# Cross-attention of a decoder layer: exponentials in place, four buffers for the scores with the top ones removed, value products transposed, and a new order of the work in every engine's step

## The reference, cut to what matters

```
q = heads(layernorm(x) @ Wq.T + bq)      # 16 heads of 32, 100 queries
k = heads(ctx @ Wk.T + bk);  v = heads(ctx @ Wv.T + bv)   # 722 keys
scores = q @ k.T / sqrt(32)
top_scores, top_idx = top_k(scores, 32)
w = softmax(top_scores)
out = sum(w * v[top_idx])
x = x + out @ Wo.T + bo
x = x + layernorm(x) @ M + bias
```

## Time and profile before

| | us |
|---|---|
| median of 3 runs | 2792.08 |
| lowest, highest | 2772.25, 2794.88 |
| profiled execution | 2798.57 |
| its span, first to last instruction | 2796.8 |
| mean granted TensorE clock of the span | 0.898 of full speed |

### The profile page before, as it was taken

How to read it: one execution, slowest core, us unless ns; L and a number is a source line. 1 busy time by engine, 2 the same in 40 slices (tenths; PEclk the granted TensorE clock), 3 DMA queues, 4 the chain that set the end, 5 groups by cost and what they waited for, 6 DMA issues and landing times. The chain is left out here.

```text
span 2796.8 us, 47371 instructions
## 1 busy us (share of the span) xinstructions
PE 2325.4 (83%) x16760; PEld 1898.0 (68%) x16760; DVE 2033.7 (73%) x3866; ACT 1411.8 (50%) x3040; POOL 1014.8 (36%) x912
## 2 busy tenths in 40 slices
PE   3788788788878758899898898898899988988987
PEld 2556556555655447787787777777778877877875
DVE  4544544554454218899899899899898988998996
ACT  3222222122222125767667667667666666666663
POOL 3344335334533122343333343343333333333421
PEclk9898898889888779999999899999999999999987
DMA  4000000000000230000000000010000000000000
GB/s 157 7 19 9 9 18 9 9 9 18 9 9 12 79 97 14 25 15 14 25 19 15 15 28 15 15 28 14 15 26 17 15 16 28 15 15 23 14 1 7
DMA packets 37617, 63.03 MB, mean 23 GB/s; under 512 B 4014, under 2 KB 20542, under 8 KB 37420
## 3 DMA queue, kind: packets, MB, share of 16 engines
q1 hardware_dynamic: 35836, 56.28, 6.7%
q0 software_dynamic: 1584, 4.30, 0.5%
HBM read 53.99 MB, written 6.55 MB: 22 GB/s over the span
## 5 line engine op out<-in xcount | busy, mean ns | idle before, releaser
L1236 DVE MATCH_REPLACE8 ca_W<-ca_top,ca_W 128x722 f32<-128x722 f32 (+1 forms) x624 | 553.4, 894 | 0.0
L1227 DVE MAX8 ca_top<-ca_W 128x8 f32<-128x722 f32 (+1 forms) x624 | 536.3, 897 | 2.6
L883 POOL TENSOR_TENSOR ca_E<-ca_E,ca_S 128x722 f32<-128x722 f32 (+1 forms) x208 | 357.3, 1738 | 306.0 <-ACT ca_S L1088 305.9
L983 PE MATMUL ca_pO<-ca_V,ca_PT 128*128 128x64 f32 (+1 forms) x2496 | 347.1, 295 | 77.5 <-ACT ca_ctxT L1127 77.2
L983 PEld LDWEIGHTS ca_pO<-ca_V,ca_PT 128*128 128x128 f32 (+1 forms) x2496 | 334.8, 207 | 104.8 <-ACT ca_PT L1110 76.3
L865 POOL TENSOR_TENSOR ca_KL<-ca_K,ca_KH 128x384 fp32r<-128x384 f32 (+1 forms) x128 | 114.0, 891 | 508.9 <-ACT ca_KH L1081 508.9
L873 POOL TENSOR_TENSOR ca_cL<-ca_raw,ca_cH 128x768 fp32r<-128x768 f32 (+1 forms) x64 | 110.5, 1726 | 337.1 <-ACT ca_cH L1064 337.1
L1215 DVE MAX8 ca_top<-ca_S 128x8 f32<-128x722 f32 (+1 forms) x208 | 181.3, 901 | 58.0 <-ACT ca_S L1105 55.4
L88 PE MATMUL ca_pF<-ca_cH,ca_WkH 128*128 128x338 f32 (+1 forms) x512 | 194.3, 380 | 22.9 <-POOL ca_cL L873 22.9
L964 PE MATMUL ca_pT<-ca_ident,ca_E 128*128 128x128 f32 (+1 forms) x1248 | 190.4, 295 | 17.0 <-POOL ca_E L883 16.9
L1088 ACT ACTIVATE ca_S<-ca_W,ca_shift 128x722 f32<-128x722 f32 (+1 forms) x208 | 185.1, 890 | 38.6 <-DVE ca_W L1236 26.3
(11 more groups left out here) (204 smaller groups left out, 5256.4 us busy)
## 6 DMA issues: line engine op xcount, KB each, us to landing
ca_raw<-in_ctxT SPq DMA_DIRECT2D x32, 384.0 KB, 3.7
ca_raw<-in_ctxT SPq DMA_DIRECT2D x32, 338.0 KB, 3.0
sa_xin<-in_x SPq DMA_DIRECT2D x16, 200.0 KB
sa_xres<-in_x SPq DMA_DIRECT2D x16, 200.0 KB
x_scratch<-sa_x SPq DMA_DIRECT2D x16, 200.0 KB
ca_xin<-x_scratch SPq DMA_DIRECT2D x16, 200.0 KB
out<-ca_x SPq DMA_DIRECT2D x16, 200.0 KB
sa_E<-in_WQ SPq DMA_DIRECT2D x12, 256.0 KB, 13.2
```

The lines of the kernel that those rows point to most:

```text
L883: pool.tensor_tensor(E[r][0:t.rows, :], E[r][0:t.rows, :], S[r][0:t.rows, :], ALU.subtract).then_inc(p_ready, 1)
L983: last = pe.matmul(out, PT[:, k, 0:t.rows], rhs, start=k == 0, stop=k == KC - 1)
L1227: n_of[t.i] = order.mark(dve.max(eight, w[rows, :]))
L1236: ins = dve.match_replace(w[rows, :], eight, (w if k else S[r])[rows, :], REMOVED)
```

## The change

- **Buffers.** `E` is gone. `exps` writes exp(S) over S, `exps_left` exp(W) over W, GpSimd subtracts W from S into S, and the transposes read S. `W` has four buffers. `exps` now needs the first MATCH_REPLACE8 of its tile to have read S (semaphore `removed`); `keep_scores` needs the transposes of the tile four back.
- **Values.** V is stationary (32 columns), PT moves; the result comes out transposed, straight in head strips of a PSUM tile, `NUM`. A product of 1/Z (broadcast over 32 columns) with the identity puts the reciprocals beside it, `DEN`. For each group of four heads `keep_output` copies both to `NR`, and one multiplication on GpSimd (`place_output`) writes `ctxT`; the rest tile's is VectorE's. `normalise`, `output_T`, `On` and `late_tile` are gone.
- **Moved to GpSimd:** the shifts (`shifts`), 1/Z as a power of -1 (`inverse`), the low half of q (`query_low`).
- **Order.** ScalarE does `exps` at the end of its step, behind the second slices. TensorE starts with the first score in every step, both tiles of `last` do their values in the same step, and the projections of x stand in the middle. Output projection s = 1, statistics s = 3, `xn` and its transpose s = 4, product with M s = 5, store s = 6; for the next batch statistics s = 1, `xn` and transpose s = 2, q s = 3, split of q s = 5. `PLAN` moves slices 4, 11 and 13 behind. `xin` is loaded ahead of the context. q has a buffer of its own, `qT`.

The diff, with 8 columns of indent taken off, without the semaphore declarations, the setup and the row work whose new place stands above, and with most removed lines cut (they stand in the kernel above):

```diff
-    PLAN = [([12, 13], []), ([], [0, 1]), ([2], [3]), ([4, 5], [6]), ([], [7, 8]), ([9], [10]), ([11], [])]
+    PLAN = [([12], [13]), ([], [0, 1]), ([2], [3, 4]), ([5], [6]), ([], [7, 8]), ([9], [10]), ([], [11])]
...
-E = [sb(f"E{r}", [128, KV]) for r in range(RING)]
-W = [sb(f"W{r}", [128, KV]) for r in range(2)]
+W = [sb(f"W{r}", [128, KV]) for r in range(RING)]
...
+def group_of(t):
+    if t.rest:
+        return GROUPS - 1
+    return t.g if t.t == 2 else None
...
-            load_context(b, 0)
+            if not tiles:
+                load_context(b, 0)
             need(sp, xn1_ready, b.count(1, 1))
             need(sp, xb_ready, b.count(1, 1))
             sp.dma_start(xin[:, :], batch_of(x1_dram, b, 1)).then_inc(x_in, 16)
+            if tiles:
+                load_context(b, 0)
             load_context(b, 1)
...
+    def shifts(tb, tp, t):
+        r, rows = ring(t, tp), slice(0, t.rows)
+        pool.wait_ge(peaked, tb.count(NT, t.i + 1))
+        settle(pool)
+        pool.tensor_scalar(shift[rows, r:r + 1], top[r][rows, 0:1], -SCALE, None,
+                           ALU.mult).then_inc(shift_ready, 1)
+    def weights(tb, tp, t):
+        r, rows = ring(t, tp), slice(0, t.rows)
+        pool.wait_ge(e_ready, tb.count(NT, t.i + 1))
+        pool.wait_ge(f_ready, tb.count(NT, t.i + 1))
+        pool.tensor_tensor(S[r][rows, :], S[r][rows, :], W[r][rows, :], ALU.subtract).then_inc(p_ready, 1)
+    def inverse(tb, tp, t):
+        r, rows = ring(t, tp), slice(0, t.rows)
+        ob, oi = before(tb, t, RING)
+        need(pool, o_mm, parts_done(ob, Tile(oi)))
+        pool.wait_ge(z_ready, tb.count(NT, t.i + 1))
+        pool.tensor_tensor(rZ[rows, r:r + 1], Z[rows, r:r + 1], minus_one[rows, :], ALU.pow).then_inc(rz_ready, 1)
+    def place_output(tb, tp, t):
+        n = group_of(t)
+        if n is None or t.rest:
+            return
+        if n == 0:
+            need(pool, y_mm, tb.count(1, 0))
+        pool.wait_ge(o_kept, tb.count(GROUPS, n + 1))
+        pool.tensor_tensor(ctxT[:, n, :], NR[:, 0, :], NR[:, 1, :], ALU.mult).then_inc(ot_ready, 1)
+    def query_low(bn):
+        pool.drain()
+        for h in range(4):
+            rows, cols = slice(DH * h, DH * h + DH), slice(T * h, T * h + T)
+            pool.wait_ge(q_hi, bn.count(5, h + 1))
+            need(pool, q_lo, bn.count(5, h))
+            pool.tensor_tensor(QL[rows, :, cols], qT[rows, :, :], QH[rows, :, cols].bitcast(F32),
+                               ALU.subtract).then_inc(q_lo, 1)
...
+            first, second = (slices(s, part, b, par, tiles, nxt) for part in range(2))
+            for x in last:
+                weights(*x)
+            for x in last:
+                inverse(*x)
+            for x in cur:
+                shifts(*x)
...
+            if s in (1, 4) and nxt:
+                context_low(bn, 2 * (s // 3) + 1)
+            if s == 5 and nxt:
+                query_low(bn)
+            for x in first + second:
+                if SLICES[x[2]][1] == "K":
+                    key_low(*x)
+            for x in last:
+                place_output(*x)
+            if s in (0, 3) and nxt:
+                context_low(bn, 2 * (s // 3))
...
+        r = ring(t, tp)
         pe.wait_ge(pt_ready, tb.count(NT, t.i + 1))
...
+        pe.wait_ge(rz_ready, tb.count(NT, t.i + 1))
         if t.i == 0:
             pe.wait_ge(kv_out, tb.count(NSL, NSL))
+        if t.rest:
+            pe.wait_ge(o_kept, tb.count(GROUPS, 3))
+        elif t.t == 0:
+            need(pe, o_kept, tb.count(GROUPS, max(t.g - 1, 0)))
+        settle(pe)
+        if t.rest:
+            n = t.rows
+            pe.matmul(pO[3 * DH:128, DEN:DEN + n], rZ[0:n, r:r + 1].broadcast_to((n, DH)), ident[0:n, 0:n],
+                      start=True, stop=True)
+            for g in range(4):
+                at = NUM + REST * g
+                for k in range(KC):
+                    last = pe.matmul(pO[3 * DH:128, at:at + REST], V[tp][:, k, 128 * g + 3 * DH:128 * g + 128],
+                                     PT[:, k, REST * g:REST * g + REST], start=k == 0, stop=k == KC - 1)
+            last.then_inc(o_mm, 1)
+            return
+        at = T * (t.g % 2)
+        for _, cols, to, g, q in t.blocks():
+            pe.matmul(pO[to:to + DH, DEN + at + q.start:DEN + at + q.stop],
+                      rZ[:, r:r + 1].broadcast_to((128, DH)), ident[:, cols], start=True, stop=True)
         for k in range(KC):
...
+            for _, cols, to, g, q in t.blocks():
+                last = pe.matmul(pO[to:to + DH, NUM + at + q.start:NUM + at + q.stop],
+                                 V[tp][:, k, 128 * g + to:128 * g + to + DH], PT[:, k, cols],
+                                 start=k == 0, stop=k == KC - 1)
+                if k == KC - 1:
+                    last.then_inc(o_mm, 1)
     def body(b, par, tiles, prev, nxt):
         bn = b.next()
         for s in range(7):
             cur, last, coming = tiles_at(s, b, par, tiles, prev, nxt)
...
+            if coming:
                 score(*coming[0])
...
             for x in slices(s, 0, b, par, tiles, nxt):
                 project(*x)
             if last:
                 weights_T(*last[0])
...
+            if s == 1 and prev:
+                pe.wait_ge(ot_ready, b.count(GROUPS, 0))
+                for c in range(CC):
+                    ins = pe.matmul(pX[0:T, :], ctxT[:, c, :], WoT[:, c, :], start=c == 0, stop=c == CC - 1)
+                ins.then_inc(y_mm, 1)
+            if s == 3 and nxt:
                 pe.wait_ge(x1T_ready, bn.count(1, 1))
                 for o in range(CC):
                     for c in range(CC):
...
                 ins.then_inc(q_mm, 1)
...
+            if s == 5 and prev:
+                pe.wait_ge(x2T_ready, b.count(1, 0))
+                for c in range(CC):
+                    ins = pe.matmul(pX[0:T, :], xT[:, c, :], M[:, c, :], start=c == 0, stop=c == CC - 1)
+                ins.then_inc(f_mm, 1)
+            if last:
+                values(*last[0])
+            if len(coming) > 1:
+                score(*coming[1])
+            if len(last) > 1:
+                weights_T(*last[1])
+            for x in slices(s, 1, b, par, tiles, nxt):
+                project(*x)
...
+            if len(last) > 1:
+                values(*last[1])
...
         r, rows = ring(t, tp), slice(0, t.rows)
+        ob, oi = before(tb, t, RING)
         act.wait_ge(picked, tb.count(NT, t.i + 1))
...
+        act.wait_ge(shift_ready, tb.count(NT, t.i + 1))
+        act.activation(W[r][rows, :], W[r][rows, :], ACT.Exp, bias=shift[rows, r:r + 1],
                        scale=SCALE).then_inc(f_ready, 1)
+        need(act, rz_ready, ob.count(NT, oi + 1))
         act.activation(top[r][rows, :], top[r][rows, :], ACT.Exp, bias=shift[rows, r:r + 1],
                        scale=SCALE, accum_out=Z[rows, r:r + 1]).then_inc(z_ready, 1)
     def exps(tb, tp, t):
         r, rows = ring(t, tp), slice(0, t.rows)
+        act.wait_ge(removed, tb.count(NT, t.i + 1))
+        act.wait_ge(shift_ready, tb.count(NT, t.i + 1))
+        act.activation(S[r][rows, :], S[r][rows, :], ACT.Exp, bias=shift[rows, r:r + 1],
+                       scale=SCALE).then_inc(e_ready, 1)
+    def keep_scores(tb, tp, t):
         ob, oi = before(tb, t, RING)
         need(act, pt_mm, ob.count(NT, oi + 1))
...
         act.wait_ge(s_mm, tb.count(NT, t.i + 1))
         act.activation(S[ring(t, tp)][0:t.rows, :], scores[0:t.rows, :], ACT.Copy).then_inc(s_ready, 1)
     def keep_weights_T(tb, tp, t):
...
+        need(act, o_mm, parts_done(tb, t, before=True))
         act.wait_ge(pt_mm, tb.count(NT, t.i + 1))
         act.activation(PT[:, :, 0:t.rows], chunks(pT[:, 0:KC * 128], KC)[:, :, 0:t.rows],
                        ACT.Copy).then_inc(pt_ready, 1)
...
+    def keep_output(tb, tp, t):
+        n = group_of(t)
+        if n is None:
+            return
+        need(act, ot_ready, tb.count(GROUPS, n))
+        act.wait_ge(o_mm, parts_done(tb, t))
+        src = pO[:, 0:4 * T].rearrange("p (a g q) -> p a g q", a=2, g=2)[:, :, n % 2, :]
+        out = NR[:, :, :]
+        if t.rest:
+            src, out = (x[3 * DH:128, :, 0:4 * REST] for x in (src, out))
+        act.activation(out, src, ACT.Copy).then_inc(o_kept, 1)
...
+            if s in (1, 4) and nxt:
+                context_high(bn, 2 * (s // 3) + 1)
+            if s == 5 and nxt:
+                need(act, s_mm, b.count(NT, NT - 1 if tiles else 0))
...
+                    act.activation(QH[rows, :, T * h:T * h + T], qT[rows, :, :], ACT.Copy).then_inc(q_hi, 1)
+                need(act, s_mm, b.count(NT, NT if tiles else 0))
+                act.activation(chunks(RH[3 * DH:128, :], 4)[:, :, 0:REST], qT[3 * DH:128, :, T - REST:T],
                                ACT.Copy).then_inc(q_hi, 1)
...
             for x in slices(s, 0, b, par, tiles, nxt):
                 keep(*x)
             if last:
                 keep_weights_T(*last[0])
...
```

(40 more changed lines are left out.)

264 lines of the change are left out of this document (67 added, 197 removed).

## The result

The changed kernel takes **2956.03 us** (median of 4 runs, 2945.27 to 2964.36), the kernel before in the same comparison 2793.48 (2772.25 to 2796.31): a ratio of 1.060, 95% interval 1.054 to 1.066. I had forecast 2828 in a range of 2640 to 2900. The direction was right, the size was not: 163 us slower where I had 36, and outside the range.

What follows compares the result with a forecast made beforehand. The ring through three queues was to bound the kernel: 106.5 us plus 4.5 for the clock, 111 a batch, 3 more than before. Fifteen batches (+45) less 9 fixed gave +36, 2835, as median 2828 us; range 2640 to 2900.

Steps and rivals of the forecast that it cites:

- VectorE, `W`, GpSimd: Cross-attention batch: VectorE's work falls to 92.3 us, its wait for `W` goes, GpSimd's work rises to 60 us.
- Values per tile: TensorE's new value product: 1.1 us for a full tile instead of 1.45, 3.0 us for the rest tile.
- rival 4: Pauses in s1, s4, s6 cost the clock (8.6 us) and strips are dear (6 x 1.0): 121 us a batch, 2975 us; chance 0.13.
- The ring: Loop through ScalarE, GpSimd and TensorE queues, closed by exps at the step's end, sets the pace while VectorE waits.
- steps 3 and 5: Ring lengths at full clock of s3, with q before the values, 16.1 us, and s5, with the spectral product, 14.6 us.
- step 4: Ring length of s4 at full clock: 17.0 us, with the second raw piece landing late and two K slices.
- I take 4.5: Clock addition to a batch: 4.3 us at the granted 0.93, 8.6 if the low level's share doubles; 4.5 chosen.
- the sum: The seven steps' ring lengths at full clock added up: 106.5 us a batch, above VectorE's 92.3.
- TensorE's 57 us: TensorE's part of the 106.5 us ring, growing by 4.3 us at the granted clock of 0.93.
- the tail: Sign from the profile before: after 3.27 us idling the tail's spectral product took 5.37 us instead of 3.68.
- the first rival: The ring is slack and VectorE paces: a batch of 96 to 101 us, 2600 to 2690 us; chance 0.25.
- the second: Second rival: the ring holds but is shorter, 107.7 us a batch, 2785 us, no change; chance 0.27.

Runs made afterwards that it cites:

- c1: Changed kernel with exps behind the second score's copy (a1) and the output projection ahead of step 1's first transposes (a3): 2879.48 us, ratio 1.034.
- c2: c1 with the q projection also moved to the head of step 4 and the product with M to the head of step 6: 2798.10 us, ratio 1.005.
- b1: Kernel before, with only exps of the current pair moved to the end of ScalarE's step: 2786.81 us, ratio 1.000.
- a1: Changed kernel with exps right behind the copy of the second score instead of at the end of ScalarE's step: 2897.26 us, ratio 1.040.
- d1: Changed kernel with the three projections moved as in c2, exps left at the end of the step: 2849.15 us, ratio 1.023.
- a9: Changed kernel with 16 dummy products in TensorE's pauses of steps 1, 4 and 6: 2886.56 us, ratio 1.039.
- a2: Changed kernel with 32 dummy products in TensorE's pauses of steps 1, 4 and 6: 2928.02 us, ratio 1.051.
- a3: Changed kernel with the output projection moved ahead of the first transposes in step 1, into TensorE's pause: 2900.20 us, ratio 1.041.
- e1: c2 with ScalarE rounding the second context piece behind the first score copy in steps 1 and 4: 2749.90 us, ratio 0.989.

## Why the prediction was wrong, point by point

- **VectorE, `W`, GpSimd:** right. 93.5 us a batch against 92.3, no wait for `W`, GpSimd 54.7 against 60.
- **Values per tile:** about right. At full clock a tile's 28 instructions take 1.3 us (2031.41 to 2032.73), forecast 1.1; the rest tile's 48 products 1.7 to 1.9, forecast 3.0 with its sums. The Trainium skill (TensorEngine Tiling (Array Packing), Key Properties) says that a change of the tiling mode drains the engine. The rows put a small bound on it: the last value product ends at 2032.81 by its row, and the score behind it starts at 2032.73; the score's second product starts 0.27 us after its first, where the later ones follow 0.17 apart. A change back costs 0.1 us at most here. So of rival 4's price the 6.0 us for dear strips did not come.
- **The ring:** right in its path, and in its length where TensorE had no pause (steps 3 and 5, within 0.3 us). In step 4 I had the second context piece in place 5.3 us into the step and `values` at 6.9; it was 5.4 and 7.1. Step 3 gave back a member's duration when q went (c1 to c2). What it lacked: it is a ring only as long as nothing else is longer, as b1 and the misses of a1, c1, c2 and d1 say.
- **The term that failed is the clock's**, "I take 4.5". The table's excess over the sum is 12.2 us a batch. a9 gave 5.2 of it back by filling three pauses, nearly all in steps 1 and 6. Another 2.6 lie in step 4 and 1.4 in step 2, where a9 leaves the products slow; the first goes away in a2's step 4, the second in a3's step 2, each time with the same products at full clock. Together 9.2 us: the 8.6 that I had put under the fourth rival, not the 4.5. My working spread the loss over TensorE's 57 us at the old mean of 0.93. But pauses and slow products aren't spread: what TensorE waits for, GpSimd's subtraction, is the release of its own part of the ring, so every slow product behind the pause is on the path. I had written that rival 4 decides where the clock goes below 0.88; it was 0.87, and 2975 us was its price; that 2956 came so near it is partly luck, since half of what that rival added was the strips, and it had no term for the next point.
- **The rest, some 3 us a batch:** 6 times in thirteen batches, at the turn of the loop, TensorE stands 2.8 us with nothing shown that it waits for, 1.3 us a batch. The kernel before has that too (17.2 us, 6 times), and my sum left it out. Of the changed kernel:

```profile
PE ca_pS L88 <- issue: 16.9, 6, 3.1
```

  Another 1.2 us lie in step 0, and its thirteen turns say where: five have a granted clock of 1.00 and take 13.7 us, against my 14.1; the eight others have 0.74 to 0.89 and take 15.1 to 18.0, six of them right behind that stop of the loop. So this too goes with the clock, as far as reading shows; no run took it away. Some 0.5 us stay open.
- **The chances:** 0.13 for a case at or near what came, and a range cut at 2900 though half of that rival was at 2890. I had listed no sign against it: nothing in the profile of before spoke for a high clock beside pauses of 4 to 5 us, and the tail, spoke for a low one. Two small slips: 15 x (-7) - 9 from 2792 gives 2678 for the first rival, not 2690, and the second comes to 2779, not 2785.

Edits interact, so their gains don't add: `exps` gave 59 us alone, 21 behind the projection (a3 to c1) and nothing in the kernel before, q and M 81 behind those, while the reciprocal gave 36 us in e1's order and nothing that can be told in the changed kernel.

## What to carry to other kernels

Sum an in-order design as a ring through its queues, step by step, and then ask where on that ring TensorE stands idle: the products right behind the pause are the ones that run slow, and they are on the path, so price them one by one at the low level and not with a mean clock. Put independent products (a projection, here) into the pause rather than behind what ends it; that takes them off the ring. It keeps the clock only if the waits that are left are short: two of 1.4 and 1.8 us were enough to lose it again in a3. A filler must be shorter than the pause. An edit that is free in one order can be worth 59 us in another, so measure each move in the order that is to be kept, and read step by step where its gain came from: a3's total was as expected, and its steps were not.

## What the runs showed of the hardware

- After an idle time of 4.6 to 4.8 us the granted clock is at the lower of its two levels (1.2 of 2.4 GHz): six transposes 1.51 us against 0.82, 23 value products 2.33 against 1.27, a score's first product 0.67 against 0.43. Behind step 1's pause of 4.83 us the level rose within the projection's 5.61 us.
- Two short waits can be followed by the low level, and need not be: 1.54 and 1.30 us around six transposes in step 2 of the changed kernel were (23 value products 1.92 us), the same two waits in a3's step 2 were not (1.09 us).
- Dummy products in a pause hold the clock as well as real ones do: six transposes take 0.85 us behind 16 of them and 1.27 us of idling, and 0.85 in a3 behind the projection and 1.41 us.
- 24 products of 32 weight columns and some 64 moving ones, in two column strips in turn, take 0.93 to 1.27 us at full clock (39 to 53 ns each, where the 96 in four strips of the earlier trace rows take 23); 48 in one strip take 1.69 us at full clock (35 ns each), here in e1_context_high:

```profile
2008.83 1.69 PE L1053 MATMUL ca_pO<-ca_PT,ca_V 128*32 128x16 f32 x48
```
